# Two causal heads scored from plain fp32 rows, value projections dealt to heads 2 to 5, and the last two feed-forwards alternating between the batches

## What is computed

```python
def _mha(x, y, wq, wk, wv, li1_w, ..., causal):       # a1: causal, y = x;  a2: y = context
    xn, yn = _ln(x, ...), _ln(y, ...)
    q, k, v = xn @ wq, yn @ wk, yn @ wv                # per head
    a = softmax(q @ k.T * D ** (-0.5))                 # over all 512 keys, then masked
    a = a * mask if causal
    x_out = x + (a @ v) @ li1_w + li1_b
    return x_out + gelu(_ln(x_out) @ li2_w + li2_b) @ li3_w + li3_b
...
x = x + tanh(g_xattn[1]) * L1_xattn(layernorm(x), ctx)
xf = layernorm(x)                                       # last: expert 7 of 8
y = (gelu(xf @ W1 + b1) @ W2 + b2) * softmax(xf @ Wr.T)[:, 7]
return x + tanh(g_ffn[1]) * y
```

## Time and profile before

| | us |
|---|---|
| median of 3 runs | 397.04 |
| lowest and highest run | 395.81, 398.46 |
| the profiled execution | 393.52 |
| its span, first to last instruction | 391.5 |

### The profile page before, as it was taken

The page is one execution under the profiler, slowest core; times in us unless marked ns, Lnnn a source line. Parts: engine busy times, 40 slices in busy tenths (PEclk is TensorE's granted clock), DMA queues, the critical chain, the costliest instruction groups (busy, mean ns, idle before and its releaser), DMA issues.

```text
span 391.5 us, 6859 instructions
## 1 busy us (share of the span) xinstructions
PE 327.2 (84%) x2134; PEld 232.9 (59%) x2134; DVE 288.1 (74%) x740; ACT 269.5 (69%) x953; POOL 121.9 (31%) x227
## 2 busy tenths in 40 slices
PE   4889998636478879898998899988957999987796
PEld 4868987413225545565655555765644788764556
DVE  0777779578869976898989989646585987945515
ACT  2478897656447997989989899516217888754060
POOL 1327574147413231332323333211112533421200
PEclk9999999966579998999999999999996999999999
DMA  6800000000039799105941984000000000000001
GB/s 215 339 3 1 2 3 0 0 1 3 0 71 214 149 202 199 28 2 120 210 102 39 211 183 163 2 2 0 2 1 0 3 2 0 3 0 0 2 0 54
DMA packets 6907, 24.74 MB, mean 63 GB/s; under 512 B 1451, under 2 KB 1528, under 8 KB 6136
## 3 DMA queue, kind: packets, MB, share of 16 engines
q1 hardware_dynamic: 6872, 24.31, 25.8%
HBM read 7.00 MB, written 0.52 MB: 19 GB/s over the span
## 4 chain that ended last, share of the span: by engine, by line
PE 46%; DVE 21%; ACT 17%; DMA 5%; issue 5%; SPq 3%; POOL 1%; DVEq 0%; ACTq 0%
PE ps L444 8%; ACT pring L1224 7%; PE ps L541 7%; PE ps L561 7%; PE ps L618 5%; PE ps L601 5%; DVE nm L1621 4%; PE ps L470 3%; SPq L863 3%; PE ps L724 3%; ACT arena L1100 3%; DVE xn L1302 3%; DMA stack<-sides 3%; PE ps L688 2%; ACT arena L1208 2%
## 5 line engine op out<-in xcount | busy, mean ns | idle before, releaser
L1621 DVE TENSOR_REDUCE nm<-ps 128x1 f32<-128x512 f32 x128 | 81.4, 680 | 16.0 <-PE ps L688 15.9
L1224 ACT ACTIVATE pring<-ps,nm 128x512 f32<-128x512 f32 x128 | 88.7, 721 | 4.3 <-DVE nm L1621 4.2
L1100 ACT ACTIVATE arena<-ps,nmx 128x77 f32<-128x77 f32 x256 | 79.1, 342 | 15.3 <-DVE nmx L1393 15.0
L988 POOL TENSOR_SCALAR_AFFINE_SELECT pring<-pring 128x128 f32<-128x128 f32 x128 | 37.1, 293 | 82.8 <-ACT pring L1224 82.8
L688 PE MATMUL ps<-stack 128*128 128x512 f32 x128 | 54.8, 490 | 6.7 <-DMA stack<-hid 3.4
L1100 ACT ACTIVATION_READ_ACCUMULATOR arena<-ps,nmx 128x1 f32 x256 | 57.1, 223 | 0.0
L953 POOL TENSOR_TENSOR arena<-arena,rden 128x616 f32<-128x616 f32 x32 | 39.2, 1224 | 52.9 <-DVE rden L1402 52.9
L444 PE MATMUL ps<-ident,pring 128*128 128x128 f32 x320 | 47.1, 277 | 7.2 <-ACT arena L1208 5.6
L444 PEld LDWEIGHTS ps<-ident,pring 128*128 128x128 f32 x320 | 37.0, 141 | 21.1 <-POOL pring L988 9.8
L561 PEld LDWEIGHTS ps<-arena 128*128 128x128 f32 x320 | 38.9, 191 | 13.2 <-DVE arena L1409 11.8
L944 POOL TENSOR_TENSOR rstd<-var,minus_half 128x4 f32<-128x4 f32 x18 | 18.4, 1022 | 89.5 <-DVE var L1295 89.5
(11 more groups left out here) (146 smaller groups left out, 517.6 us busy)
## 6 DMA issues: line engine op xcount, KB each, us to landing
stack<-sides SPq DMA_DIRECT2D x32, 256.0 KB, 4.9
stack<-arena SPq DMA_DIRECT2D x16, 256.0 KB, 5.0
stack<-hid SPq DMA_DIRECT2D x12, 256.0 KB, 5.1
wa_sb<-in_wa SPq DMA_DIRECT2D x1, 1536.0 KB, 13.6
early<-in_w SPq DMA_DIRECT2D x2, 512.0 KB, 7.2
stack<-hid SPq DMA_DIRECT2D x8, 128.0 KB, 2.5
arena<-in_wa SPq DMA_DIRECT2D x1, 1024.0 KB, 4.8
pring<-in_wf SPq DMA_DIRECT2D x1, 768.0 KB, 9.7
```

The lines of the kernel that those rows point to most:

```text
L988: pool.affine_select(out=blk, in_=blk, compare_op=ALU.is_gt, fill=0.0, base=0, pattern=[[1, P]], channel_multiplier=-1).then_inc(masked, 1)
L1100: ins = act.activation(Pc[:, i % PC_SLOTS, h * HS:h * HS + M], bank(where[key])[:, h % 4 * HS:h % 4 * HS + M], ACT.Exp, bias=nmx[:, i % 4, ...
L1224: release(act.activation(pring[:, n % 2, i, :], bank(f"S{i}"), ACT.Exp, bias=nm1[:, n % 8, i:i + 1], accum_out=den1[:, n % 8, i:i + 1]), ( ...
L1621: dve.tensor_reduce(nm1[:, n % 8, i:i + 1], bank(f"S{i}"), AX.X, ALU.max, negate=True).then_inc(nm1_ready, 1)
```

## The change

In the attention, heads 0 and 1 no longer use the stack. DVE writes a plain fp32 copy of projections 0 to 3 (`plain_copy`) into the first 32 rows of `sides`, ahead of each low half, and PE multiplies these; the first stack transfers are those of j = 1, after four low halves. The value projections of batch 0 go from before the loop and n = 0 to the ends of n = 2 to 5, with banks by `next_T`; their copies are dealt to n = 2 and 4 (ACT) and n = 3 and 5 (DVE). Projections 4 to 7 come one each at n = 1 to 4. `ln1_bias(1)` goes into n = 0 and `ln_stats("a1", 1)` to n = 1 on DVE; PE's a1 transposes of batch 1 go to n = 5, and ACT's evacuations between the second and third exponential of n = 6. POOL's code is the same. `normalise` and the bank of the first `sums_transposes` follow from this.

In the tail `ffn` is split in `ffn_up` and `logits`, and PE does: up a2f 0, transposes a2f 1, down a2f 0, up a2f 1, half of down a2f 1, transposes f1 0, the other half, up f1 0, logits 0, half of down f1 0, transposes f1 1, the other half, up f1 1, logits 1, down f1 1. ACT and DVE follow that order; `a2_residual` does what `bias_and_residual` and the products behind it did, one batch at a time. Hunks that only rename or pass an argument are left out.

```diff
-            if n in (0, 2):
-                return [(4 + n, "B"), (5 + n, "A")]
+            if 1 <= n <= 4:
+                return [(3 + n, "AB"[n % 2])]
...
+        def plain(which):
+            return sides[0:D1, "qk".index(which), :, :]
...
-                if i == 0:
-                    if n < 2:
-                        pe.wait_ge(first_stack[n], 16 * 4)
-                    elif e == 0:
-                        t = n // (2 * HG)
-                        pe.wait_ge(stacked[j], stack_count(t, j))
...
+                if n < 2:
+                    if i == 0:
+                        pe.wait_ge(plain_ready, 2 * n + 2)
+                    filled(pe.matmul(bank(f"S{i}"), plain("q")[:, e, i * P:(i + 1) * P], plain("k")[:, e, :],
+                                     start=True, stop=True), ("s1", n, i))
+                    return
+                if i == 0 and e == 0:
+                    t = n // (2 * HG)
+                    pe.wait_ge(stacked[j], stack_count(t, j))
...
-                res = "A" if k < NGRP - 1 else "B"
+                res = "B" if k == NGRP - 1 else "A" if k else next_T()
...
-            for t in range(2):
-                project_values(t, f"T{t % 2}")
...
-                if n == 0:
-                    project_values(2, "T0")
...
-                if n == 0:
-                    project_values(3, "T1")
...
+                if n == 5:
+                    ln_transposes("a1", 1)
...
-                if n == 4:
-                    ln_transposes("a1", 1)
+                if 2 <= n < 2 + NT:
+                    project_values(n - 2, next_T())
...
-            ffn("a2f", 0)
+            ffn_up("a2f", 0)
             ln_transposes("a2f", 1)
-            ffn("a2f", 1)
             ffn_down("a2f", 0)
-            ffn_down("a2f", 1)
+            ffn_up("a2f", 1)
+            ffn_down("a2f", 1, range(0, 2))
+            ln_transposes("f1", 0)
+            ffn_down("a2f", 1, range(2, NT))
             pe.wait_ge(loaded["wf1"], 16)
-            ln_transposes("f1", 0)
-            ffn("f1", 0)
+            ffn_up("f1", 0)
+            logits(0)
+            ffn_down("f1", 0, range(0, 2))
             ln_transposes("f1", 1)
-            ffn("f1", 1)
-            ffn_down("f1", 0)
+            ffn_down("f1", 0, range(2, NT))
+            ffn_up("f1", 1)
+            logits(1)
             ffn_down("f1", 1)
...
-            for e in range(2):
-                sp.wait_ge(lo_ready, 2 * e + 2)
-                stack_up(0, 0, e, e + 1, first_stack[e])
...
-            copy_values(0)
...
+                    if u == 0 and n == 6:
+                        a1_evac(1)
+                if n in (2, 4):
+                    copy_values(n - 2)
                 if n >= HG and n % HG == 1:
                     sums_across(n // HG - 1)
-                if n == 5:
-                    a1_evac(1)
...
-            for site, names in (("a2f", ("a2_ln3_g", "a2_ln3_b")), ("f1", None)):
-                if site == "a2f":
-                    preload(ACT.Gelu)
-                else:
-                    ln_evac(site, 0, names)
-                gelu(site, 0, names)
-                gelu(site, 1)
+            preload(ACT.Gelu)
+            gelu("a2f", 0)
+            ln_evac("a2f", 1, ("a2_ln3_g", "a2_ln3_b"))
+            gelu("a2f", 1)
+            for b in range(NB):
+                ln_evac("f1", b)
+                gelu("f1", b)
...
+            def a2_residual(b, step):
+                if step == 0:
+                    did(dve.tensor_tensor(xb[:, b, :, :], x1[:, b, :, :], row4("a2_li3_b"), ALU.add))
+                elif step == 1:
+                    did(dve.tensor_tensor(xb[:, b, :, :], xb[:, b, :, :], xo[:, b, :, :], ALU.add))
+                else:
+                    did(dve.scalar_tensor_tensor(r[:, b, :, :], xb[:, b, :, :], tg[:, 1:2], r[:, b, :, :],
+                                                 ALU.mult, ALU.add))
+                settle()
...
+            def plain_copy(m):
+                which, e, _ = projection(m)
+                dve.wait_ge(hi_ready, m + 1)
+                src = bank(await_bank(dve, ("qk", m)))[0:D1, :]
+                dve.tensor_scalar(plain(which)[:, e, :], src, float(D1) ** -0.5 if which == "q" else 1.0, None,
+                                  ALU.mult).then_inc(plain_ready, 1)
...
-            low_half(0)
-            ln1_bias(1)
-            for m in range(1, 4):
+            for m in range(4):
+                plain_copy(m)
                 low_half(m)
-            copy_values(1)
...
+                if n in (3, 5):
+                    copy_values(n - 2)
                 if n == 0:
-                    copy_values(3)
+                    ln1_bias(1)
+                if n == 1:
                     ln_stats("a1", 1, x1)
...
-            bias_and_residual("a2_li3_b")
-            for b in range(NB):
-                did(dve.scalar_tensor_tensor(r[:, b, :, :], xb[:, b, :, :], tg[:, 1:2], r[:, b, :, :],
-                                             ALU.mult, ALU.add))
-            settle()
...
+            for step in range(3):
+                a2_residual(0, step)
+            a2_out(0)
+            ln_stats("f1", 0, r)
+            for step in range(3):
+                a2_residual(1, step)
+            ln_norm("f1", 0, r)
+            a2_out(1)
+            ln_stats("f1", 1, r)
+            ln_norm("f1", 1, r)
```

More of the change, by code:

```diff
@@ L602, in ffn, with logits @@
                            ("up", site, b, k))
-                if site == "f1":
-                    claim(pe, "T0", ("logits", b), read_by=(logits_ready, b + 1))
-                    for t in range(NT):
-                        m = pe.matmul(bank("T0")[:, t * 8:(t + 1) * 8], xnT[:, b, t * P:(t + 1) * P],
-                                      wf1_sb[:, 2 * HID:2 * HID + 8], start=True, stop=True)
-                    filled(m, ("logits", b))
+            def logits(b):
+                claim(pe, "T0", ("logits", b), read_by=(logits_ready, b + 1))
+                for t in range(NT):
+                    m = pe.matmul(bank("T0")[:, t * 8:(t + 1) * 8], xnT[:, b, t * P:(t + 1) * P],
+                                  wf1_sb[:, 2 * HID:2 * HID + 8], start=True, stop=True)
+                filled(m, ("logits", b))
             def ffn_down(site, b, tiles=range(NT)):
@@ L1242, in _ @@
             preload(ACT.Gelu)
[L1243 removed]
+            gelu("a1f", 0)
             gelu("a1f", 1)
```

44 lines of the change are left out of this document (16 added, 28 removed).

## The result

| | before | after |
|---|---|---|
| median, 20 runs each | 395.02 | 399.20 |
| lowest and highest | 393.15, 398.46 | 396.43, 401.02 |
| the profiled execution | 393.52 | 399.46 |
| its span | 391.5 | 397.6 |
| its mean granted clock (of full speed) | 0.952 | 0.930 |

The ratio is 1.010, with an interval of 1.0076 to 1.0125. The forecast was 395.3 with 399.0 as its upper end.

What follows compares the result with a forecast made beforehand. No single bound: VectorE and TensorE near full nearly everywhere. Span 391.5 - 0.4 (attention) - 1.3 (tail) = 389.8; the same 1.7 off the median 397.04 gave 395.3, range 392.0 to 399.0.

Steps and rivals of the forecast that it cites:

- DVE's start: Entry to attention: DVE begins head 0 at 115.8 instead of 118.03, 2.2 us earlier.
- POOL's hold: Heads 1 and 2: POOL takes a1's power before head 1's masks, delaying transposes; DVE idles about 1.95 us, bounds 0.9 to 3.
- The stack of tile 1: Before head 8: transfers start about 143.5, land at 150.9, head 8 asks about 152.4; hidden by 1.5 us.
- The tail: Last two feed-forwards: reordering ends the kernel 1.3 us earlier, bounds 0.4 and 2, with the routing chain still last.
- rival (d): Tail: if PE and not the routing chain set the end, 3.6 us gained, total 393.0; chance 0.05.
- DVE is busy 31.35 ... After: 115.8 + 31.35 + 1.75 + ...: Attention up to head 8: start, busy time, new work and idles reach 154.1 against 154.48, 0.4 us earlier.
- hidden too: Head 1: PE's 5.3 us of scores, transposes and projection end at 122.5, covered by DVE's work to about 122.75.
- (b): Heads 2 to 5: PE's waits near 124 halve its clock, total 397 to 400.3, middle 398.7; chance 0.1.
- heads 3 to 5: Value projections taking turns in T0/T1 delay the next head's second transposes: 0.85 us idle in all, between 0 and 2.
- the gain near head 7: Heads 6 and 7: moving the a1 evacuation leaves 2.4 us of DVE idle against 4.97 before, bounds 1 and 4.
- the bounds -3 to +2 and -2 to -0.4: Time changes in us allowed for attention and for the tail, given as a total of 392.0 to 397.
- clock 1.00 at 146 to 149: Sign near head 7: PE's granted clock stays full there, where before it was 0.54 in 146.10 to 149.60.

Runs made afterwards that it cites:

- rows128: after, with POOL clearing `sides` and k copied with 128 rows, so plain products run over 128 rows with zeros in q; ratio to before 1.0027.
- exp_early: tail_only with logits 1 inside f1 0's down products, small exponentials before the last four GELUs and a second GELU table load; ratio 0.9883, median 390.17.
- power_late: after, with POOL's power of ("a1", 1) behind head 1's masks instead of head 0's; ratio to before 1.0068.
- rows_power: after, with both the edit of rows128 and that of power_late; ratio to before 0.9980.
- tail_only: before with the change's new tail alone, attention as before; ratio to before 0.9956.
- plain_32: before with the new tail and plain heads 0 and 1 over 32 rows, value projections where before has them; ratio 0.9997.
- plain_rows: tail_only plus heads 0 and 1 from plain rows over 128 rows, value projections left in place; ratio to before 0.9961.
- values_back: after, with value projections 0 and 1 put back ahead of the loop, 32-row plain products still following each other; ratio to before 1.0146.
- deal_only: tail_only plus value projections, their copies and projections 4 to 7 dealt as in after, heads 0 and 1 still stacked; ratio to before 1.0033.

## Why the prediction was wrong

**Right, step by step.** DVE's start: 115.8 forecast, 116.14 measured, from a first projection that itself came 0.31 later. Plain copies: 0.60 from start to start behind each other, 0.68 long, taken at 0.6. POOL's hold: forecast 1.95 of DVE's time, and at full clock DVE's two waits in rows128 make 1.99, ACT's wait 1.8; timed 1.9 in one pair and 1.3 in the other; the row that was to show it, a mask at the heels of the power and PE behind POOL, is there, 3.6 us later than forecast in after and on time in rows128 (124.14 for 124.3). The stack of tile 1 never held PE; its transfers began at 148.36, not 143.5, and head 8 asked later as well. The loop from head 8 on unchanged: 90.65 for 90.62. The tail: 1.3 forecast, 1.33 measured, with the routing chain last and no wait before the last operations; exp_early, which takes that chain away, gains, so rival (d) is out.

**Wrong: the clock.** The step that failed is the sum "DVE is busy 31.35 ... After: 115.8 + 31.35 + 1.75 + ...", which took PE at full clock in heads 1 and 2 and called head 1's scores "hidden too". PE was hidden only at full clock. In after it is busy 13.16 of the 14 us in which the clock is 0.53, and DVE waits for it. I had a rival with a fallen clock, (b), but it tied the fall to PE's *waits* near 124, gave it 0.1, and measured its danger by an idle of before. PE did wait in head 2, for 0.84 from 128.4 on, but the clock had fallen by 120. What took the clock away was the part that I had priced with most care, 16 instructions over 32 rows: their time was right, and what they do to the clock was in no row of before, which has no product over 32 rows there at all. The chance of the rival should have had that unknown in it.

The size of it, timed: 2.9 us from after to rows128 and 3.5 from power_late to rows_power, where the single traces show 6.4 (54.11 less 47.73, 1.2 of it ahead of the plain products) and 4.1. As the mean clocks of the runs show, the profiled execution of after had one of the lowest clocks of its runs and that of rows128 the highest of its.

**Also off: what is moved.** rows128 shows the sum with the clock at 1.00 all the way from DVE's start to head 8. There DVE is busy 33.54 us where the sum has 33.1 (31.35 and 1.75). It is idle 6.5 where the sum has 5.2: 1.99 behind POOL's hold (forecast 1.95), 1.29 in heads 3 to 5 (0.85), 2.52 before head 7 and 0.46 in it (2.4 together), and 0.2 in small pieces. Start to head 8 takes 40.04 for 38.3, so this part was 1.7 too short; the start itself came 0.8 sooner after the first projection than forecast. In all it is 47.73 from the first projection, 0.6 behind before, where the forecast was 0.4 ahead.

The term that was read wrongly is the gain near head 7. The sum sets 2.4 against the 4.97 of before, but those 4.97 hold a fall of the clock. With the attention of before and the clock at 1.00 (exp_early) the same two waits are 2.96 and 0.46, 3.42 together, against 2.98 in rows128: the gain is 0.4 and not 2.6.

With both faults mended, rows_power is at head 8 0.35 us ahead of before (46.80 for 47.15) in its trace, but before has that fall and rows_power doesn't. Against exp_early (45.84) it is 0.96 behind, which agrees with the timed runs: its ratio is 0.0024, 0.95 us, above tail_only, with overlapping intervals. Its DVE starts 2.5 us sooner after the first projection than in exp_early (8.56 for 11.03), and takes 3.4 more from there to head 8 (38.24 for 34.81). So even without its two faults the attention part of the change is no gain that these runs show.

The range had a slip of its own: the bounds -3 to +2 and -2 to -0.4 give 398.6 as the upper end, not 397. The sign "clock 1.00 at 146 to 149" came true in after by its words only, since the fall had moved to 154 with the work.

**The whole, in us of the timed runs** (ratios times 395.02): tail -1.7; plain start, dealing and the rest +0.95; POOL's hold +1.9; the clock +2.9; together +4.0, and 399.20 less 395.02 is 4.2. These are steps of one chain of ratios (tail_only, rows_power, rows128, after), so that they add up is no proof of the single ones; by way of power_late POOL's hold is 1.3 and the clock 3.5. Behind the steps of 0.95 and 1.9 stand overlapping intervals. The forecast was -0.4 and -1.3 against a median of 397.04 that itself lay 2.0 above the 395.02 of more runs; against that one it would have been 393.3, and the error is 5.9.

**Still open.** Whether it is the number of rows alone: rows128 also changes what stands in them (zeros beside q) and clears `sides` on POOL. What 32 rows cost without a fall of the clock is seen in traces only: in plain_32 a group of four instructions takes 1.90 us from its start to that of the next kind (114.94 to 116.84), in plain_rows over 128 rows 1.71 (115.52 to 117.23). Four groups make 0.8, and plain_32 is 0.8 behind plain_rows at head 8 (49.73 and 48.94); timed they differ by 0.0036 on different chips with overlapping intervals. Open too is what decides whether PE's wait of 1.91 near head 7 is followed by a fall of the clock or not, in the same code.

## What to carry to other kernels

When a change puts work on a PE stretch that is only just hidden, ask what it costs at half the clock, and look at the *kind* of products as well as at the idle: here products over 32 of 128 rows in a row lost the clock with PE full, and the same products with wider ones between them, or widened with zeros, did not. Work that seems free at a wait (the value projections in the stack wait) may be what keeps the clock; price its removal, not only its new place. When an order is changed on one engine, walk the queue of each engine that reads from it: POOL's unchanged code cost 1.9 us in one pair of runs and 1.3 in another. And before a wait is booked as a gain, look at the clock behind it: of the 4.10 before head 7 1.1 were the clock's.

## What the runs showed of the hardware that was not expected

- PE's granted clock can fall to 0.50 while PE is busy without a wait. In after it was 1.00 up to 119 and 0.50 from 120 to 133, with PE busy 6.32 of 6.44 us up to 119.00, from 113.86 on in 32-row products; in power_late and values_back the same (busy 6.44 of 6.44 in the latter), in rows128, rows_power and plain_32 not. The Trainium skill, "TensorE: Matmul & The Clock Gate", What's actually happening, says that activity releases the throttle; by that, the fuller PE should have the better clock. The trace agrees for the idle of deal_only (3.83, with 0.66 in 119 to 126) and not for after, where the profile shows PE busier before the fall than in rows128.
- Plain fp32 products that follow each other take the same time over 32 rows as over 128 (weights loaded every 0.43 us in after and in rows128, twice a product), so widening them with zeros is free, up to a clear of the buffer. Between 128-row products a pair of 32-row ones takes 0.19 more (1.90 for 1.71 us).
- One and the same wait of PE, 1.91 us, was followed by 0.50 in before and tail_only and by 1.00 in exp_early. So the same code gives traces up to head 8 that differ by 1.29 us (45.84 and 47.13), and behind head 31 by over 3: a part under 1 us is told from one trace only against another with the same clock, or from timed runs.
